# Splitting down blocks one set ahead in the first phase, with another order of the closing products

## What is computed

```
x = x + 0.5 * ffn(layernorm(x), w_gate, w_up, w_down)
x = x + scan_block(layernorm(x), W, lam_logit, eta, gamma, beta)
x = x + 0.5 * ffn(layernorm(x), w_gate, w_up, w_down)

ffn(x):        down( silu(x @ w_gate.T) * (x @ w_up.T) )
scan_block(x): z = x @ W.T;  m_t = lam * m_(t-1) + z_t  for four lam
               h = z + sum(eta * m);  gamma * normalised(h) + beta
```

## Time and profile before

| | |
|---|---|
| median of 3 runs | 1025.92 us (1024.21 to 1026.52) |
| the profiled execution, whole | 1023.93 us |
| its span, first to last instruction | 1022.2 us |
| TensorE busy | 1010.2 us, 99% |
| VectorE, ScalarE, GpSimd busy | 70%, 42%, 19% |
| granted TensorE clock, mean of the span | 1.000 |
| moved by DMA | 224.21 MB, 219 GB/s over the span; 300 to 360 GB/s from 50 to 200 us |

### The profile page before, as it was taken

One profiled execution on the slowest core, in us unless ns is written; L12 is line 12 of the kernel. 1 busy time (PEld: TensorE's weight loads), 2 busy tenths in 40 slices (PEclk: granted clock), 3 DMA queues, 4 the chain that ended last, 5 costly groups with the idle time before them and its releaser, 6 DMA issues.

```text
span 1022.2 us, 13275 instructions
## 1 busy us (share of the span) xinstructions
PE 1010.2 (99%) x4796; PEld 849.0 (83%) x4796; DVE 720.5 (70%) x1063; ACT 426.6 (42%) x681; POOL 193.1 (19%) x219
## 2 busy tenths in 40 slices
PE   8999999999999999999999999999999999999998
PEld 7778888877888888888888888888888888888998
DVE  7856685689888787866977887786586444454753
ACT  6645555547333632313824344232273332333530
POOL 4443365306300200210412020003040000000000
PEclk9999999999999999999999999999999999999999
DMA  6589998888666644646756764554577645554255
GB/s 206 205 320 348 358 343 299 311 273 258 231 234 231 221 145 165 208 150 226 250 181 221 234 223 161 180 168 145 182 267 242 216 166 200 209 178 165 94 182 179
DMA packets 73617, 224.21 MB, mean 219 GB/s; under 512 B 6481, under 2 KB 24913, under 8 KB 65873
## 3 DMA queue, kind: packets, MB, share of 16 engines
q1 hardware_dynamic: 72976, 222.33, 63.1%
q10 hardware_dynamic: 576, 1.05, 0.3%
HBM read 168.82 MB, written 54.53 MB: 219 GB/s over the span
## 4 chain that ended last, share of the span: by engine, by line
PE 92%; DVE 3%; DMA 2%; issue 1%; ACT 1%; SPq 1%; POOL 0%; DVEq 0%; ACTq 0%
PE ps_a L1779 8%; PE ps_a L1780 8%; PE ps_a L1781 8%; PE ps_b L1779 7%; PE ps_b L1780 7%; PE ps_b L1781 7%; PE ps_d L1779 7%; PE ps_d L1781 7%; PE ps_d L1780 7%; PE ps_c L1781 6%; PE ps_c L1780 6%; PE ps_c L1779 6%; PE aux L1779 3%; PE aux L1780 3%; PE aux L1781 3%; DMA t_kept<-zx 1%
## 5 line engine op out<-in xcount | busy, mean ns | idle before, releaser
L1203 DVE TENSOR_TENSOR tmp<-tmp,ps_c 128x512 f32<-128x512 f32 x59 | 40.4, 685 | 120.5 <-PE ps_c L1781 120.5
L1779 PE MATMUL ps_a<-xt,gu 128*128 128x512 f32 x304 | 118.4, 390 | 0.6 <-ACT tmp L707 0.6
L1780 PE MATMUL ps_a<-xt,gu 128*128 128x512 f32 x304 | 118.3, 389 | 0.0
L1781 PE MATMUL ps_a<-xt,gu 128*128 128x512 f32 x304 | 118.3, 389 | 0.0
L1779 PE MATMUL ps_b<-xt,gu 128*128 128x512 f32 x286 | 111.5, 390 | 1.3 <-ACT tmp L680 1.3
L1780 PE MATMUL ps_b<-xt,gu 128*128 128x512 f32 x286 | 111.3, 389 | 0.0
L1781 PE MATMUL ps_b<-xt,gu 128*128 128x512 f32 x286 | 111.3, 389 | 0.0
L1779 PE MATMUL ps_d<-dn,hid 128*128 128x512 f32 (+1 forms) x256 | 92.9, 363 | 0.5 <-DVE hid L1248 0.5
L1781 PE MATMUL ps_d<-dn,hid 128*128 128x512 f32 (+1 forms) x256 | 92.8, 363 | 0.0
L1780 PE MATMUL ps_d<-dn,hid 128*128 128x512 f32 (+1 forms) x256 | 92.8, 362 | 0.0
L1781 PE MATMUL ps_c<-xt,gu 128*128 128x512 f32 x236 | 91.8, 389 | 0.0
(11 more groups left out here) (272 smaller groups left out, 2321.2 us busy)
## 6 DMA issues: line engine op xcount, KB each, us to landing
dn<-dn_kept SPq DMA_DIRECT2D x92, 512.0 KB, 3.9
gu<-gu_kept SPq DMA_DIRECT2D x46, 1024.0 KB, 5.1
gu<-gu_kept SPq DMA_DIRECT2D x46, 768.0 KB, 5.1
gu_kept<-gu SPq DMA_DIRECT2D x14, 1024.0 KB, 5.7
gu_kept<-gu SPq DMA_DIRECT2D x14, 768.0 KB, 4.2
dn_kept<-dn SPq DMA_DIRECT2D x16, 512.0 KB, 5.2
t_kept<-zx SPq DMA_DIRECT2D x16, 512.0 KB, 5.8
dn<-t_kept SPq DMA_DIRECT2D x16, 512.0 KB, 3.6
```

What stands on the lines that cost most here:

```text
L1203: dve.tensor_tensor(dst, u3s(si), p5_bank(si)[:, :], ALU.add).then_inc(c22_done, 1)
L1779: pe.matmul(dst, a_hi, b_hi, start=start, stop=False, skip_group_check=chained)
L1780: pe.matmul(dst, a_hi, b_lo, start=False, stop=False, skip_group_check=chained)
L1781: return pe.matmul(dst, a_lo, b_hi, start=False, stop=stop, skip_group_check=chained)
```

## The change

In phase 0 each down block is split one set earlier (block si+1 in set si; blocks 2 and 3 both in set 2), and its raw load is issued one turn earlier from k = 3 on. GpSimd makes the sums of pair 0 at k = 2 as before, those of pair 1 at k = 3 (before 4), pair 2 at 5 (before 6), and so on up to pair 7 at 15 (before 16). The sums are split in the sets of `T_SETS`, before in (2, 4, 6, 8, 10, 12, 14, 15). SyncE stores pair 0 at k = 3, pair 1 at 5, pair 2 at 7, and so on up to pair 6 at 15, behind the loads of its turn, and pair 7 right after the loop, ahead of the fetches of the `down1` weights. At the end of phase 3 the batches run in the order of `ENDING`. The counts that products wait for, VectorE's adds and two of the stores follow it.

```diff
+    ENDING = ([(Q5, 0), (Q5, 1)] + [(Q6, i) for i in range(4)] + [(Q5, 2), (Q5, 3)]
+              + [(w, i) for w in (Q7, Q3, Q4) for i in range(4)])
+    T_SETS = (2, 4, 5, 7, 9, 11, 13, 14)
+    ENDED = (Q6, Q5, Q7, Q3, Q4)
```

SyncE, in its loop over k, behind it, and at the end of the program:

```diff
                 keep_dn(k - 1)
-                if k + 1 < HT:
+                if k < 4:
                     load_dn_raw(k + 1)
+                if 2 < k < HT - 2:
+                    load_dn_raw(k + 2)
...
-                if k >= 4 and k % 2 == 0:
-                    keep_t(k // 2 - 2)
-
-            keep_t(6)
+                if k == 3:
+                    keep_t(0)
+                if k > 4 and k % 2:
+                    keep_t((k - 3) // 2)
+
+            keep_t(7)
             sp.wait_ge(dn_stored[0], 16 * 4)
             fetch_dn(16)
...
             keep_dn(15)
-            keep_t(7)
...
             sp.wait_ge(block_added, 10)
+            sp.dma_start(out_v[3, :, :, HALF:D], x_tok[:, 12:16, HALF:D]).then_inc(out_stored, 16)
+            sp.wait_ge(block_added, 12)
             store_tile(2)
-            sp.wait_ge(block_added, 12)
-            sp.dma_start(out_v[3, :, :, HALF:D], x_tok[:, 12:16, HALF:D]).then_inc(out_stored, 16)
```

ScalarE, in set si of phase 0; VectorE's `before_c12` is changed in the same way, with `dn_lo_of` and `t_lo_of`:

```diff
-                        dn_hi_of(si)
-                        if si % 2 == 0:
-                            t_hi_of(si // 2 - 1)
-                        if si == 15:
-                            t_hi_of(7)
+                        if si == 2:
+                            dn_hi_of(2)
+                        if si < 15:
+                            dn_hi_of(si + 1)
+                        if si in T_SETS:
+                            t_hi_of(T_SETS.index(si))
```

GpSimd, in its loop over k from 2 to 16:

```diff
                 sums(k)
-                if k % 2 == 0 and k <= SETS:
-                    t_sums_of(k // 2 - 1)
+                if k == 2:
+                    t_sums_of(0)
+                if k % 2:
+                    t_sums_of(k // 2)
```

VectorE and TensorE, the ending:

```diff
             for n in range(5, 20):
                 stage_lo_of(n)
-                if n % 4 == 1:
-                    add_product(n // 4 - 1)
+                if n in (7, 9, 13, 17):
+                    add_product({7: Q6, 9: Q5, 13: Q7, 17: Q3}[n])
...
-                    pe.wait_ge(block_added, {Q6: 2, Q3: 6, Q7: 8, Q4: 12}[w])
+                    pe.wait_ge(block_added, {Q6: 2, Q3: 8, Q7: 6, Q4: 10}[w])
...
-            for w in (Q5, Q6, Q3, Q7, Q4):
-                for i in range(4):
-                    batch(w, i)
+            for m in range(len(ENDING)):
+                batch(m)
```

More of the change, by code:

```diff
@@ L498, in fetch_dn @@
                 else:
-                    w, i = divmod(n - SEG - PAIRS, 4)
+                    w, i = ENDING[n - SEG - PAIRS]
                     if n == SEG + PAIRS:
@@ L899, in stage_hi_of @@
             def stage_hi_of(n):
-                w, i = divmod(n, 4)
+                w, i = ENDING[n]
                 if n < len(STAGES):
@@ L1333, in add_product @@
             def add_product(w):
[L1335 to L1338, removed]
+                banks, tile, half, added = {Q5: (z_ps, 3, 1, 0), Q6: (x_ps, 2, 1, 0), Q3: (z_ps, 2, 1, 6),
+                                            Q7: (x_ps, 3, 1, 8), Q4: (x_ps, 3, 0, 0)}[w]
+                add_block(banks, 0, tile, half, bank_done, ENDED.index(w) + 1, added)
+                add_block(banks, 1, tile, half, batch_done, ENDING.index((w, 3)) + 1, added)
             def zw_lo_of(j):
@@ L1565, in before_c12 @@
                     gu_lo_b(si + 1)
[L1566 to L1570, removed]
+                    if si == 2:
+                        dn_lo_of(2)
+                    if si < 15:
+                        dn_lo_of(si + 1)
+                    if si in T_SETS:
+                        t_lo_of(T_SETS.index(si))
                     if 5 <= si < 9:
@@ L1948, in first_block, with batch @@
                 last.then_inc(first_done, 1)
-            def batch(w, i):
-                m = 4 * w + i
+            def batch(m):
+                w, i = ENDING[m]
                 n = SEG + PAIRS + m
```

## The result

The changed kernel took **1031.4 us** (median of four runs, 1029.59 to 1032.67) beside 1025.1 for the kernel before: ratio 1.0072, 95% interval 1.006 to 1.0085. Run again with the last experiments: 1.0068 [1.0055, 1.0081]. It is slower by 6.3 us, where 2.7 was forecast. The profiled execution took 1029.59 us, the shortest of the four, with a span of 1027.8.

The account below looks back on a forecast made before the run. TensorE's work plus its idle moments was taken to bound the kernel. 9.1 us added less 6.4 saved gave +2.7 on a median of 1025.9, so 1028.6 us; the range was 1024.5 to 1031.8.

Parts of the forecast that it names:

- rival 1: TensorE's clock falls in one or both new waits: 2 us for one fall, 4 for two (1030.6 to 1032.6); chance 0.2.
- (a): Set 5: ScalarE's split of pair 1 no longer waits for pair 0's store to land; 1.5 us saved.
- (b): Set 15: VectorE no longer splits a down block and a pair first, so `lo0(15, 1)` comes earlier; 0.7 us saved.
- (c): Waits at 227 and 231: pair 7's earlier store lets VectorE's row start sooner; 2.6 us saved, plus 0.5 after 250.
- (d): Ending, near 1007: TensorE no longer waits behind an output add, as `Q4` follows `Q3`; 1.1 us saved.
- (e): Set 3: GpSimd's sums of pair 1 delay `sums(4)`, so TensorE waits for `copy_u2(3)`; 3.5 us added.
- (f): Sets 14 and 15: ScalarE's split of pair 7 waits for pair 6's store, delaying `copy_p1(15)`; 4.4 us added.
- (g): Ending: batch 2, now `Q6`'s first, also waits for the two adds of `x_ps`; 1.2 us added.
- The sum as it stands: Main case, whole kernel: saved and added waits net +2.7 us, giving 1028.6, with no fall of the clock; chance 0.52.
- The prediction's own sign of being wrong: No wait of TensorE above 2 us before 210, or PEclk below 1 behind one, would show the forecast wrong.

Follow-up runs that it names:

- ending: The kernel before the change with only the new order of the last batches and its counts; 1024.54 us, ratio 0.9999.

## Why the prediction was off

The direction and the range held. The size did not: 6.3 in place of 2.7.

That 1031.4 lies in the range is in part luck. The range reached to one fall of the clock, and two came: rival 1 in its full form, whose own figure was 1032.6. And the 1025.9 that the forecast was added to was the median of three executions; with a fourth it was 1025.1, and 1024.3 to 1024.4 in the groups later.

Matmul by matmul, the trace after against that of before gives the sum again. Saved: (a) 1.5, (b) 0.7, (c) 2.8 and the 0.6 near 250, (d) 1.1, together 6.7 (forecast 6.4). Added: (e) 3.9, (f) 4.5, (g) 1.2, together 9.6 (forecast 9.1). The slow matmuls 3.4 (forecast 0). TensorE gained 0.6 ahead of set 3, 0.5 of it at the program's start, by chance. 9.6 - 6.7 + 3.4 - 0.6 = 5.7, as the two profiled executions differ.

- **(a)** No wait is left in set 5. Its price differs by execution: 1.3 in one profile, 2.0 and a fall of the clock in another. The 1.5 taken fits the first; which length is usual isn't shown, but most executions of the kernel before have a clock of 1.000.
- **(b), (d)** Gone, as costed; (d) with (g), forecast at +0.1, measured -0.1 [-1.0, 0.8] by `ending`.
- **(c)** Shown to hang on pair 7's store. Put back, it costs 3.9, more than the 2.6 to 3.1.
- **(e)** 3.5 forecast; 3.9 and 4.2 in the two profiles. The chain was the one forecast, each link within 0.2: `sums(4)` ended at 54.6, the copy at 56.7. TensorE had come to it 0.6 sooner, which made the wait so much longer.
- **(f)** 4.4 forecast; 4.5 in both. The chain was right, with the start at 207.1 in place of 205.5: later by about what set 3 had lost to the clock.
- **(g)** 1.2 forecast; 1.3 in the profile.
- **The clock.** This is the step that failed. "The sum as it stands" got 0.52 and the fall of the clock 0.2. The sum put it at nothing. The clock fell in both waits and took 1.7 us each time in the profiled execution: 2.7 + 3.4 = 6.1, beside the 6.3 of the medians. The prediction's own sign of being wrong, a PEclk below 1 behind a wait, came true twice. The size of a fall, priced at 2, was about right (1.5 to 3.0 in the sixteen falls that the traces hold, ends of programs aside). Its chance was wrong. The argument against was that the clock fell at the end of the trace only after 2.6 to 3.3 us, and that the waits end "soon after such a time". But by that row both waits, of 3.5 and 4.4, were longer than the time to the fall, so the row spoke for two falls, not for none. That no wait of the kernel before was above 1.3 was wrong as well: the one for `hid` was 1.7, also at a clock of 1.00. The forecast held an absence of evidence (no slow matmul in the trace of before) against a rule that the only row bearing on it supported. The section that was named, "Why this matters for your kernels" on the page "TensorE: Matmul & The Clock Gate" of the Trainium skill, warns against just such gaps. The runs agree with the warning, and half of the time at the lower clock is lost: at a mean clock of 0.59, 3.3 of the 4 us from 57 to 61 were at 1.2 GHz. They differ in the length: the clock fell behind gaps of 1.9 to 2.2 us too, shorter than those that the section warns against, and there the measurement decides.

With the clock at its full chance the forecast would have been 1028.6 + 4 = 1032.6, against 1031.4; added to the 1025.1 it is 1031.8.

## What to carry to other kernels

A wait of the engine that bounds a kernel has two prices: its length, and what the clock takes behind it. Here waits of 2.0 us and more cost 1.5 to 3.0 on top in every trace, whatever their length, so a wait that is only shortened may give back far more or less than the part cut off. When an edit moves work ahead in an in-order list, look at the first instruction behind it that the bounding engine needs: here two of the moves put a landing or a slower engine in front of TensorE's next operand. Such an edit should be undone piece by piece before it is judged, since the whole was slower by 6 and, with those two undone, faster by 5.

## What was not expected of the hardware

- The clock fell behind a wait of 2.0 us and not behind one of 1.4, nor at the program's start behind 1.7 and 1.8 of idle time. It did not always fall at once: with 11 filler matmuls TensorE started again at 58.13, and its starts became 0.43 apart only from 59.5 on. In four of seven executions of that kernel it fell, in three it didn't.
- The two falls cost 3.4 in the profiled execution of the changed kernel, but others of it had a lower mean clock (0.994, 0.995) and took 1.1 to 3.1 us more. They have no trace, so where it was down longer is open.
- Filler matmuls of 128x128 were priced at 0.33 us from the start of the program (18 in 5.9 us). In the waits they took 0.23 (18 in 4.2). A price from one stretch did not hold in another, since half of the first stretch ran at another pace. In the kernel before:

```profile
1.60:4.80 3.20, 3.20 (x15) 1.00 0.79 292
4.90:6.90 2.00, 2.00 (x20) 1.00 1.07 391
```

The starts lie 0.21 apart up to 4.9 and 0.11 from then on, the same factor of two as in the slow stretches. The view gives a clock of 1.00 for both, so that it was the clock there too is likely and not shown.
